# Gating the first of four couples on GpSimd instead of VectorE, in a fused Mamba-2 and mixture-of-experts kernel

## What is computed

```
zxbcdt = rmsnorm(x) @ Win            # z, (x, B, C), dt
xBC = silu(conv4(xBC));  dt = softplus(dt + dt_bias)
h_t = exp(dt * -exp(A_log)) * h + (x*dt) outer B        # state, step by step
y = einsum(h, C) + D * x
y = y * silu(z)                      # the gate
x = x + rmsnorm(y, gnorm) @ Wout
```

## Time and profile before

| | |
|---|---|
| median of three runs | 1144.78 us |
| the profiled execution: its time | 1150.03 us |
| its span, first to last instruction | 1148.2 us |
| PE, DVE, ACT, POOL busy | 85, 76, 67, 32% of the span |
| the 24 blocks | about 45 to 960 us |
| `weigh` on VectorE (L1743) | 300.3 us in 192 |
| `gate_y` on VectorE (L1763) | 66.1 us in 96 |
| `square_y` on GpSimd (L571) | 109.1 us in 96 |
| POOL idle until a gate has come | 274.7 us |

### The profile page before, as it was taken

One profiled execution on the slowest core, in us unless ns is written; L12 is line 12 of the kernel. 1 busy time (PEld: TensorE's weight loads), 2 busy tenths in 40 slices (PEclk: granted clock), 3 DMA queues, 4 the chain that ended last, 5 costly groups with the idle time before them and its releaser, 6 DMA issues. The chain is left out here.

```text
span 1148.2 us, 47596 instructions
## 1 busy us (share of the span) xinstructions
PE 972.6 (85%) x20326; PEld 573.8 (50%) x20326; DVE 873.9 (76%) x1372; ACT 763.8 (67%) x1486; POOL 369.1 (32%) x410
## 2 busy tenths in 40 slices
PE   4889888988899898888989898888899876877797
PEld 2455444554455454545545454544555443456664
DVE  5789877987789788777988789777988787652255
ACT  3777777787778876787778777776887652322122
POOL 8522131321322312223223231232232213634725
PEclk9899999999999999999999999999999986879789
DMA  3411110201011001011011110101110021335621
GB/s 74 143 43 32 33 32 16 47 9 31 16 32 42 16 16 25 27 33 37 10 25 33 32 36 3 32 20 31 39 36 14 15 68 33 102 79 146 154 66 40
DMA packets 113226, 49.31 MB, mean 43 GB/s; under 512 B 85688, under 2 KB 106488, under 8 KB 113016
## 3 DMA queue, kind: packets, MB, share of 16 engines
q1 hardware_dynamic: 99544, 40.49, 13.8%
q0 software_dynamic: 3072, 3.15, 1.1%
q10 hardware_dynamic: 10400, 2.62, 1.0%
HBM read 23.62 MB, written 9.44 MB: 29 GB/s over the span
## 5 line engine op out<-in xcount | busy, mean ns | idle before, releaser
L1743 DVE TENSOR_TENSOR em<-em,gs 128x1536 f32<-128x1536 f32 (+1 forms) x192 | 300.3, 1583 | 10.1 <-ACT em L1360 9.5
L1360 ACT ACTIVATE em<-ring 128x512 f32<-128x512 f32 x480 | 248.8, 598 | 25.6 <-PE ring L1025 21.1
L1045 PE MATMUL ybank<-em,xdt 64*32 64x64 f32 (+1 forms) x12288 | 181.7, 238 | 32.6 <-issue 30.0
L1045 PEld LDWEIGHTS ybank<-em,xdt 64*32 64x32 f32 x12288 | 151.6, 106 | 94.9 <-issue 63.3
L571 POOL TENSOR_TENSOR ysq<-yg 128x512 f32<-128x512 f32 x96 | 109.1, 1136 | 278.4 <-DVE yg L1763 274.7
L1025 PE MATMUL ring<-rt,lt 128*64 128x512 bf16 x960 | 148.3, 398 | 21.0 <-ACT em L1360 12.1
L578 POOL TENSOR_TENSOR x_t<-on,x_b 128x256 f32<-128x256 f32 x48 | 41.8, 871 | 202.0 <-DVE on L1771 202.0
L1771 DVE TENSOR_TENSOR on<-oss,rr 128x256 f32<-128x256 f32 x96 | 40.4, 421 | 81.8 <-ACT rr L1370 76.9
L1750 DVE SCALAR_TENSOR_TENSOR yt<-xs,col,ybank 128x256 f32<-128x256 f32 x192 | 82.9, 472 | 23.7 <-PE ybank L1045 23.5
L1025 PEld LDWEIGHTS ring<-rt,lt 128*64 128x64 bf16 x960 | 45.1, 110 | 107.3 <-issue 42.4
L578 POOL TENSOR_TENSOR x_b<-on,x_b 128x256 f32<-128x256 f32 x48 | 35.0, 730 | 195.3 <-DVE on L1771 195.3
(11 more groups left out here) (266 smaller groups left out, 1839.0 us busy)
## 6 DMA issues: line engine op xcount, KB each, us to landing
rt<-wcat SPq DMA_DIRECT2D x80, 96.0 KB, 1.9
x_b<-x_t SPq DMA_DIRECT2D x48, 128.0 KB
cm<-bc SPq DMA_DIRECT2D x24, 224.0 KB, 2.7
rt<-lt SPq DMA_DIRECT2D x120, 24.0 KB
sorted_y<-yt ACTq DMA_DIRECT2D x10, 256.0 KB, 3.1
sorted_x<-h_b SPq DMA_DIRECT2D x4, 512.0 KB, 4.4
cw<-in_L_conv_t_cw SPq DMA_DIRECT2D x6, 320.0 KB
cw<-in_L_conv_b_cw SPq DMA_DIRECT2D x6, 320.0 KB
```

Source lines behind the costliest of these rows:

```text
L1045: mm = pe.matmul(ybank[QUAD * q:QUAD * (q + 1), ab, to:to + hi - lo], xdt[m % 2][rows, 8 * (i % 2) + 4 * first + q, r, :], em[rows, p % EM ...
L1360: emptied(act.activation(em[:, p % EM_SLOTS, :, HALF * j:HALF * (j + 1)], o.rearrange("p (h t) -> p h t", h=HEADS), ACT.Exp), "seg", n, i, ...
L1743: dve.tensor_tensor(e, e, gs[n % 2][:, i:i + 1, 0:wide].to_broadcast([P, HEADS, wide]), ALU.mult).then_inc(s_w, 1)
```

## The change

GpSimd gates couple 0 of each block itself, with its own instruction in front of the square; VectorE's instruction for it is taken away. A new semaphore `s_yg0` counts these couples, s_yg now counts only the other three of each block, and the places that waited on s_yg wait on three quarters of the number, or on both. `add_skip(k, 2)`, which writes the buffer that the first couple used, now waits for `s_yg0`.

```diff
+            def gate_first(k):
+                m = 4 * k
+                pool.wait_ge(s_yf, m + 1)
+                pool.wait_ge(s_zs, k + 1)
+                if m >= 2:
+                    pool.wait_ge(s_o, m - 1)
+                pool.tensor_tensor(out=yg[0][:].rearrange("p u t -> p (u t)"), in0=yt[0][:], in1=zs[k % 2][:, 0:4 * T],
+                                   op=ALU.mult).then_inc(s_yg0, 1)
+
             def square_y(k, c):
                 m = 4 * k + c
-                pool.wait_ge(s_yg, m + 1)
+                if c == 0:
+                    pool.wait_ge(s_yg0, k + 1)
+                else:
+                    pool.wait_ge(s_yg, 3 * k + c)
...
             for k in range(NBLOCK):
                 if k:
                     add_x(k - 1, 3)
+                gate_first(k)
                 square_y(k, 0)
...
-            pool.wait_ge(s_yg, 4 * NBLOCK)
+            pool.wait_ge(s_yg, 3 * NBLOCK)
...
-                    sp.wait_ge(s_yg, 4 * 2 * (g - 1))
+                    sp.wait_ge(s_yg, 3 * 2 * (g - 1))
...
-                    act.wait_ge(s_yg, 4 * (n - 1))
+                    act.wait_ge(s_yg, 3 * (n - 1))
...
             def add_skip(k, c):
                 m = 4 * k + c
                 dve.wait_ge(s_y, 2 * m + 2)
+                if c == 2:
+                    dve.wait_ge(s_yg0, k + 1)
...
             def gate_y(k, c):
                 m = 4 * k + c
                 dve.wait_ge(s_yf, m + 1)
-                if c == 0:
+                if c == 1:
                     dve.wait_ge(s_zs, k + 1)
...
                 weigh(k, 3)
                 if k == LAST:
                     first_sum()
-                gate_y(k, 0)
                 if more:
                     h_of(n, 1)
                 x_dt(k, 2)
```

More of the change, by code:

```diff
@@ L261, in build @@
             "x_turned", "xdt_ready", "weighed", "y_ready", "y_bank_read", "y_gated", "y_squared"))
+        s_yg0 = sem("first_couple_gated")
         s_o, s_lnr, s_r, s_on, s_x = (sem(n) for n in ("o_ready", "log_var", "r_ready", "o_normed", "x_updated"))
```

## The result

The changed kernel takes **1155.44 us** (median of 6 runs, 1150.25 to 1158.91), the kernel before, beside it, 1146.18 (6 runs): a recorded ratio of 1.0073, 95% interval [1.0042, 1.0104], which is 8.4 us of 1146.18 [4.8, 11.9]; the two medians by themselves lie 9.3 apart. It is slower. The forecast was 1147.9 in a range of 1142.0 to 1151.5: sign right, size too small, the time outside the range.

The account below looks back on a forecast made before the run. No engine's busy time alone was taken to price the change; the end of `h_of(n, 1)` was on the path. A delay of 0.24 us in 13 blocks gave 3.1, added to 1144.8: 1147.9 us, range 1142.0 to 1151.5.

Parts of the forecast that it names:

- I take 1.04, the row of the same shape: POOL's new gate running alone was priced at 1.04 us, like the square, between bounds of 1.03 and 1.23.
- a dearer gate: Rival: the gate takes 1.23 us or hides nothing, delaying 0.43 to 0.52 a block, 5.6 to 6.8 us; chance 0.15.
- exclusion and order: DVE and POOL exclude each other on SBUF: `weigh(k, 3)`, then gate, then `h_of`; the later one hides about 0.13 us.
- W: The end of `weigh(k, 3)` on DVE in a block, from which the forecast counts its times.
- The end of `h_of(n, 1)` is on the path: PE waits for `h_of(n, 1)` before `project_dt`, on which all of block n hangs; idle 0.71 us in block 14.
- DVE runs without idle time into `bias_dt`: The other way a block passes the delay on: DVE's queue has no gap up to `bias_dt`, as in block 20.
- 13 blocks: Blocks 0, 1, 4, 7, 8, 11, 13, 14, 15, 17, 18, 20, 21 pass on 0.24 us each, 3.1 us.
- the other ten: Blocks expected to swallow 0.24: 2, 3, 6, 9, 16, 10 through rstd waits; 5, 12, 19, 22 through PE stops.
- start `h_of` at W - 0.08: After the change DVE starts `h_t` at W - 0.08, held behind POOL's gate, ending at W + 1.45.
- free sharing: Rival: POOL's gate runs beside `weigh` holding nothing up, `h_of` 0.60 earlier, 3.2 us less, 1141.6; chance 0.13.
- swallowed: Rival: PE's issue stops and rstd waits absorb the delay in other blocks too, 0 to 1.5 us, 1145.5; chance 0.22.
- At nothing: Parts priced at zero, like new semaphore waits; the square's 0.24 delay is hidden, as `project_out(k, 0)` comes several steps later.

Follow-up runs that it names:

- the second: The changed kernel measured again, unchanged, against the kernel before: 1152.67 us against 1147.92, ratio 1.0044 [1.0019, 1.0069].
- the one-tensor kernel: The changed kernel, but POOL's gate multiplies yt by itself instead of by zs: 1150.18 us, ratio 1.0008 to the kernel before.
- the fill: The changed kernel, but POOL fills yg with the constant 0.5 instead of gating, reading nothing: 1149.90 us, ratio 1.0011 to the kernel before.
- `x_dt` moved ahead: The kernel before, with `x_dt(k, 2)` in front of `h_of(n, 1)` in VectorE's queue (also called `x_dt` first): 1161.73 us, ratio 1.0129.
- VectorE's gate moved behind: The kernel before, with VectorE's gate of couple 0 moved behind `h_of(n, 1)`: 1153.89 us, ratio 1.0058.
- one and a half: The changed kernel, but POOL's first instruction multiplies 768 columns of xs by zs into a scratch tile instead of gating: 1162.08 us, ratio 1.0123.
- another couple: The changed kernel, but POOL gates couple 2 instead of couple 0 and VectorE gates the others: 1146.43 us, ratio 0.9991 to the kernel before.
- half: The changed kernel, but POOL gates only 256 of the first couple's 512 columns, the others left out: 1146.13 us, ratio 0.9980 to the kernel before.
- the one kernel that delays the square by 2.9: The changed kernel, but POOL's gate also waits until `h_of(n, 1)` is written: 1165.35 us, ratio 1.0120 to the kernel before.

## Why the prediction was wrong

**The step that failed** is "I take 1.04, the row of the same shape". The gate takes 1.27, and the 0.23 of difference passes undiminished into the delay: 0.48 instead of 0.24 a block, 13 x 0.49 = 6.4 us instead of 3.1 (0.48 in the block shown, 0.49 as the median of the 13). The rival called a dearer gate (1.23 us, 5.6 to 6.8 in all, chance 0.15) was the true case. The row of the same shape reads one tensor twice; rows of two different tensors were there: `add_x`, 256 elements, 0.73, and the preparation of weights, 640, 1.53. A line through the two gives 0.73 + 256 x 0.80 / 384 = 1.26 at 512 (from the other form of `add_x`, 0.87 in the page, 1.31). I had set the broadcast patterns of the second against it, without a row that shows what these cost. The Trainium skill (GPSIMD Engine Reference, "Elementwise — side-by-side cycle accounting"), whose figure for two inputs I had quartered to an estimate of 1.12, would have missed as well; the measured 1.27 decides.

**The second part of the miss is the base.** The forecast was built on the 1144.78 of three runs. The medians of before beside the later kernels were 1146.18 to 1148.78, 1.4 to 4.0 us above. Against the kernel before, as it ran beside the change, the forecast was +3.1, and +8.4 and +5.1 were measured. The measured 1155.44 is 7.5 us above the forecast of 1147.9: 1.4 is the base, 3.3 the gate, and the 2.8 left lie within the interval of the first measurement; the second does not show them.

**Right: exclusion and order.** `weigh(k, 3)` first and of its usual length, the gate behind it, `h_of` behind the gate: shown in all 23 blocks, and by the one-tensor kernel to 0.01 us (W + 0.90, 1.45 and 1.93, against 0.90, 1.45 and 1.92). That a VectorE instruction with two SBUF inputs holds up a POOL instruction that reads SBUF, and not one that only writes, as the Trainium skill has it (SBUF — State Buffer, "Who interferes with whom"), is what the fill shows too; that the later one hides 0.13 to 0.14 holds for both gates whose own time was measured, 1.27 and 1.04.

**Right: the path.** "The end of `h_of(n, 1)` is on the path" and "DVE runs without idle time into `bias_dt`" are both shown, the first by `x_dt` moved ahead, the second by VectorE's gate moved behind.

**Right: 13 blocks.** Two kernels with a delay of about 1.05 a block give 14.1 and 14.8 us, or about 14 blocks, with intervals of 10 to 17 and 12 to 16. The traces also say which: from W of a block to W of the next, against the trace of before, the 13 listed blocks together grow by 5.4 and 5.0 us in the two traces of the change, by 15.2 with one and a half and by 12.6 with `x_dt` first; the other ten change by -0.7, -2.4, -3.2 and -0.8. In the two kernels without a delay, another couple and half, the 13 change by -1.8 and -0.6 and the ten by 0.2 and -3.6, so some 2 to 4 us of such a sum is the difference between profiles. As a group, then, the listed blocks pass the delay on and the others don't; for single blocks this stays open.

**Wrong without harm.** I let DVE start `h_of` at W - 0.08. In nine of the 13 blocks it starts at W + 0.26 to 0.47, when ACT's rstd comes, in block 0 at 0.02, in 7, 11 and 13 at 0.74 to 1.05: the gate on DVE had covered that wait. POOL's gate, until W + 1.12 or later, was still in front of it each time. But it would have cut free sharing, the rival that gained: VectorE's gate moved behind makes `h_of` only 0.10 earlier, not 0.60.

**The other rivals.** Free sharing fell with the hold-up in every block; swallowed, with the rise of the time from one length of the gate to the next.

**At nothing: as forecast** for the square. The trace of before, then that of after, from the view of waits (what waits for what: us in total, times, longest):

```profile
PE oss L1057 <- POOL ysq L571: 26.7, 29, 4.4
PE ring L912 <- DVE h_b L1648: 4.1, 9, 0.8
PE ring L912 <- DVE h_t L1648: 0.9, 3, 0.3
```

```profile
PE oss L1071 <- POOL ysq L584: 29.3, 31, 4.4
PE ring L926 <- DVE h_b L1662: 7.7, 9, 1.3
PE ring L926 <- DVE h_t L1662: 4.4, 9, 0.8
```

PE's waits for ysq grew by 2.6 us in all, no more than in the kernel of another couple, where the first square is not later at all (29.4 us in 32). In the one kernel that delays the square by 2.9 they grew by 19.7. PE's waits for the second `h_of`, of both kinds, are the rows that answer to the forecast: 5.0 us in 12 before, 12.1 in 18 after. The 7.1 more stand beside the 13 x 0.49 = 6.4.

## What to carry to other kernels

Price an operation that the trace doesn't have by rows with the same kind of operands, not only the same shape: here two different tensors cost 22% more than one read twice, and that alone doubled the delay. Before moving work to an idle engine, ask which instruction it will stand beside and which queue it will then hold up; the same gate cost 5 to 8 us beside VectorE work with two SBUF inputs and nothing measurable two couples later. And where two ways meet at one instruction, count the delay there, as the start of `bias_dt` here: an earlier input is worth nothing if the queue in front of it grows.

## What the runs showed of the hardware

- POOL's 128x512 fp32 multiplication: 1.27 us with two tensors, 1.04 with yt read twice. With yg read twice, started under the end of another, 1.09 is recorded, of which 0.04 is overlap. 256 and 768 columns of two tensors come to an estimated 0.73 and 1.82, worked out from when they end behind a VectorE instruction.
- A fill of 128x512 on POOL, which reads nothing, takes 0.53 us beside a VectorE multiplication with two SBUF inputs, in all 24 blocks.
